# A vision tower with a mixture of experts on one core: gate stores moved ahead, the first expert's weights loaded in two parts, two bias additions later, and identity matmuls in TensorE's pauses

## What is computed

```python
h = tok(x)                       # 64 images: 36 patches of 768 -> layernorm -> 256 -> layernorm, class row, positions
h = h + attention(layernorm(h))  # 37 rows of an image see each other, each row but itself
h = h + ffn(layernorm(h))        # 8 experts, 2 per row, capacity 444

# ffn
probs = softmax(x @ router_w + router_b); topv, topi = top_k(probs, 2); topv /= topv.sum()
prio = where(topi.flat == e, topv.flat, -1); pv, pp = top_k(prio, 444)   # for each expert: its 444 best rows
xin = x[pp // 2]; w = pv
out_e = (gelu(xin @ w1[e] + b1[e], exact) @ w2[e] + b2[e]) * w
out[tok] += out_e; out = layernorm(out) * ln_g + ln_b
```

## Time and profile before

| | us |
|---|---|
| median of 3 runs | 414.99 (413.75 to 417.43) |
| profiled execution, its own time | 417.57 |
| its span | 415.7 |
| granted TensorE clock, mean over the span | 0.917 |
| TensorE busy | 348.5 (84%) |
| VectorE busy | 319.1 (77%) |
| ScalarE busy | 254.7 (61%) |
| GpSimd busy | 222.5 (54%) |

### The profile page before, as it was taken

One profiled execution on the slowest core, in us unless ns is written; L12 is line 12 of the kernel. 1 busy time (PEld: TensorE's weight loads), 2 busy tenths in 40 slices (PEclk: granted clock), 3 DMA queues, 4 the chain that ended last, 5 costly groups with the idle time before them and its releaser, 6 DMA issues.

```text
span 415.7 us, 7904 instructions
## 1 busy us (share of the span) xinstructions
PE 348.5 (84%) x2128; PEld 307.8 (74%) x2128; DVE 319.1 (77%) x874; ACT 254.7 (61%) x552; POOL 222.5 (54%) x377
## 2 busy tenths in 40 slices
PE   2799999999999998540038999999999999999960
PEld 0588888887888886230028899999999999999950
DVE  7674778878888877879887655878787878787954
ACT  3255587767868775644700378686868686868620
POOL 4154776666666764430004443057777777645675
PEclk9898999999999999955557699999999999999996
DMA  6641024545454389678812386655858595852221
GB/s 174 188 88 37 30 58 129 147 128 139 126 151 135 95 134 118 163 196 248 39 0 68 115 254 187 184 147 149 231 165 249 151 243 168 244 171 76 62 83 45
DMA packets 49278, 57.29 MB, mean 138 GB/s; under 512 B 12248, under 2 KB 38229, under 8 KB 49244
## 3 DMA queue, kind: packets, MB, share of 16 engines
q1 hardware_dynamic: 42602, 43.11, 40.0%
q0 software_dynamic: 5568, 13.00, 12.0%
q10 hardware_dynamic: 1074, 0.79, 0.7%
HBM read 36.74 MB, written 21.36 MB: 140 GB/s over the span
## 4 chain that ended last, share of the span: by engine, by line
PE 56%; issue 10%; SPq 8%; POOL 8%; DMA 7%; DVE 6%; ACT 3%; ACTq 0%; DVEq 0%; POOLq 0%
PE pz L977 18%; PE pall L994 17%; PE pall L837 5%; DMA x_rows<-gate 5%; PE pall L805 3%; PE pall L812 3%; SPq L456 2%; SPq L450 2%; POOL nrm L1609 2%; PE pall L1005 1%; DMA stage<-in_x 1%; PE pall L963 1%; SPq L509 1%; PE pall L821 1%; PE pz L785 1%
## 5 line engine op out<-in xcount | busy, mean ns | idle before, releaser
L994 PE MATMUL pall<-halves 128*128 128x444 f32 x384 | 88.5, 365 | 0.8 <-DVE halves L1398 0.8
L977 PE MATMUL pz<-halves 128*128 128x444 f32 x384 | 89.1, 368 | 0.0
L977 PEld LDWEIGHTS pz<-halves 128*128 128x128 f32 x384 | 73.6, 192 | 5.0
L994 PEld LDWEIGHTS pall<-halves 128*128 128x128 f32 x384 | 70.8, 188 | 6.0 <-DVE halves L1398 1.1
L1649 POOL DMA_INDIRECT held<-x_rows,gidx x32 | 35.8, 1119 | 64.3 <-issue 50.4
L738 ACT ACTIVATE wproj<-pz,b1t 128x444 f32<-128x444 f32 x64 | 40.5, 633 | 45.3 <-PE pz L977 44.7
L1398 DVE TENSOR_TENSOR halves<-wproj,halves 128x444 fp32r<-128x444 f32 x64 | 39.8, 622 | 28.2 <-ACT halves L750 22.1
L837 PE MATMUL pall<-halves 128*112 128x256 f32 x396 | 56.6, 299 | 3.2 <-DVE halves L1089 3.2
L837 PEld LDWEIGHTS pall<-halves 128*112 128x112 f32 x396 | 51.3, 183 | 5.1 <-DVE zbias L1108 2.4
L1673 POOL DMA_INDIRECT out<-rows,didx x28 | 37.0, 1323 | 22.7 <-DVE rows L1446 15.4
L750 ACT CAST halves<-wproj 128x444 fp32r<-128x444 f32 x64 | 36.1, 564 | 2.0
(11 more groups left out here) (283 smaller groups left out, 716.4 us busy)
## 6 DMA issues: line engine op xcount, KB each, us to landing
stage<-in_w SPq DMA_DIRECT2D x32, 512.0 KB
stage<-in_x SPq DMA_DIRECT2D x64, 108.0 KB
x_rows<-x SPq DMA_DIRECT2D x22, 224.0 KB, 3.1
x_rows<-held SPq DMA_DIRECT2D x22, 224.0 KB, 4.2
sums<-rows SPq DMA_DIRECT2D x7, 448.0 KB
out<-held SPq DMA_DIRECT2D x21, 111.0 KB
x_rows<-zero SPq DMA_DIRECT2D x1, 1474.9 KB
wproj<-in_w_proj ACTq DMA_DIRECT2D x1, 768.0 KB
```

Of the source, the lines that this page charges most:

```text
L977: m = nc.tensor.matmul(bank(k % 2)[:, 0:CAP], w[:, c, k * 128:(k + 1) * 128], xs[:, e % 2, c, 0:CAP], start=(n == 0), stop=(n == 3 * EC - 1))
L994: m = nc.tensor.matmul(pall[:, 2 * (e % 2) + o, 0:CAP], w[:, k, o * 128:(o + 1) * 128], hs[:, k % 2, 0:CAP], start=(k == 0 and n == 0), st ...
```

## The change

1. SP stores the first 16 tiles' gates at the head of step 25 (TILES + 3), ahead of that step's three stores, and no longer behind the weights.
2. SP loads the first halves of w1 and w2 of expert 0 at the head of step 26, ahead of the last two tiles' `hb` and output stores. The last six tiles' gates are stored after the pipeline; the second halves of w1 and w2 follow them.
3. GpSimd adds the bias row (L1624) for tiles 18 and 19 in step 23; for tiles 20 and 21 in step 26, after a new wait for `r_V` = 2. Before, it did 18 in step 23, 19 and 20 in step 25, and 21 in step 26.
4. TensorE multiplies the identity (128x128, fp32, results into a bank that nobody reads then) 4, 5 + 2, 3 and 8 times in steps 22 to 25, 24 times between L906 and L912, 10 times ahead of the search, 9 times behind each of its first seven rounds, 2 times behind L922, 17 times behind L927, and 16 times (before: 24) behind L932.

```diff
 # SP, in step(i, slot), ahead of the stores
+                if isinstance(i, int) and i == TILES + 3:
+                    sp.wait_ge(r_V, 1)
+                    store_gates(0, EARLY)
+                if isinstance(i, int) and i == TILES + 4:
+                    sp.wait_ge(x_n, TILES)
+                    sp.wait_ge(xT_ps, TILES)
+                    sp.wait_ge(z_ps, TILES)
+                    load_w1(0, 0)
+                    load_w2(0, 0)
...
 # SP, after the pipeline
-            for h in range(2):
-                load_w1(0, h)
-                load_w2(0, h)
-            for a, b, n in ((0, EARLY, 1), (EARLY, TILES, 2)):
-                sp.wait_ge(r_V, n)
-                store_gates(a, b)
+            sp.wait_ge(r_V, 2)
+            store_gates(EARLY, TILES)
+            load_w1(0, 1)
+            load_w2(0, 1)
...
 # TensorE
+            def keep_clock(n, b):
+                for _ in range(n):
+                    nc.tensor.matmul(bank(b)[:, 0:128], ident[:, :], ident[:, :], start=True, stop=True)
...
+                if isinstance(i, int) and i >= TILES:
+                    keep_clock({TILES + 1: 5, TILES + 2: 3, TILES + 3: 8}.get(i, 0), 0)
...
+                if isinstance(i, int) and i >= TILES:
+                    keep_clock({TILES: 4, TILES + 1: 2}.get(i, 0), 0)
...
+            keep_clock(24, 6)
             for t in range(TILES - EARLY):
...
+            keep_clock(10, 7)
             for r in range(NR):
                 pe.wait_ge(r_won, r + 1)
                 nc.tensor.matmul(bank(r % 2)[:, 0:1], grp[:, :], won[:, :], start=True, stop=True).then_inc(r_n, 1)
+                keep_clock(9 if r < NR - 1 else 0, 7)
             pe.wait_ge(r_pick, 1)
             nc.tensor.matmul(bank(2)[0:P, 0:E], onesf[:, 0:P], thrrow[:, :], start=True, stop=True).then_inc(r_thr, 1)
+            keep_clock(2, 7)
...
             nc.tensor.matmul(bank(3)[0:P, 0:n], below[0:P, 0:P], gev, start=True, stop=True).then_inc(r_pos, 1)
+            keep_clock(17, 7)
...
-            keep_clock(24)
+            keep_clock(16, 7)
             for h in range(2):
                 first_gathered(h)
                 lists(h)
...
 # GpSimd, in step(i, slot)
-                for t in range(i - 6, i - 4) if isinstance(i, int) and i == TILES + 3 else (i - 5,):
-                    if live(t) and not (isinstance(i, int) and i == TILES + 2):
+                if isinstance(i, int) and i == TILES + 4:
+                    pool.wait_ge(r_V, 2)
+                for t in {TILES + 1: (i - 5, i - 4), TILES + 2: (), TILES + 3: (), TILES + 4: (i - 6, i - 5)}.get(i, (i - 5,)) \
+                        if isinstance(i, int) else (i - 5,):
+                    if live(t):
```

More of the change, by code:

```diff
@@ L475, in _, with load_w1, load_w2 @@
                 load_x(t, t)
+            HALF_H, HALF_K = HID // 2, HC // 2
+            def load_w1(e, h):
+                cols = slice(h * HALF_H, (h + 1) * HALF_H)
+                sp.dma_start(w1r[:, :, cols], w1[e].rearrange("(c p) h -> p c h", p=128)[:, :, cols])\
+                    .then_inc(w1_in[h], 16)
+            def load_w2(e, h):
+                ks = slice(h * HALF_K, (h + 1) * HALF_K)
+                sp.dma_start(w2r[:, ks, :], w2[e].rearrange("(k p) o -> p k o", p=128)[:, ks, :])\
+                    .then_inc(w2_in[h], 16)
             def step(i, slot):
                 par = slot % 2
+                if isinstance(i, int) and i == TILES + 3:
[7 more added lines that the diff above has]
+                    load_w2(0, 0)
                 t = i + 4
@@ L934, in _ @@
             m.then_inc(r_list, 1)
-            def keep_clock(n):
-                for _ in range(n):
-                    nc.tensor.matmul(bank(3)[:, 0:128], ident[:, :], ident[:, :], start=True, stop=True)
             def lists(h):
```

## The result

The changed kernel takes 423.76 us (median of 6 runs, 422.45 to 425.37), the kernel before, run beside it, 414.37: the ratio is 1.0238 (95% interval 1.0199 to 1.0277), 2.4% slower. One of the six executions of the kernel before took 1890.57 us, which nothing here explains; the other five took 411.26 to 417.43. The forecast was 416.4 with a range up to 420.2. The profiled execution took 422.45 with a span of 420.5.

What follows compares the result with a forecast made beforehand. The gate stores held the first gather by 2.0 us, with the search behind. Round 4 +2.8, products +1.4, sums -0.3, L922 and L926 -0.5, gate wait -2.0 gave +1.4 us: 416.4, range 409.8 to 420.2.

Steps and rivals of the forecast that it cites:

- When w1's half lands: On SP's queue, w1's first half lands at 200.5: pieces through at 198.3, plus 2.2 for stores and weights.
- rival 2: Gate pieces, stores and weights land all in series, w1 at 204: +4.9 us, time 419.9; chance 0.18.
- Round 4: In the search, ScalarE waits for w1, so this round's sum comes at 202.8, +2.8 us.
- The products at half clock: On TensorE, the clock falls in the pause; nine products behind round 4 make round 5 late by +1.4 us.
- Full clock on the later sums: In the search, three later sums get shorter at full clock, -0.3 us; L922 and L926 give a further -0.5.
- The gate wait: Ahead of GpSimd's first gather, the wait for the gate stores goes, giving 2.0 us.
- The sum: Over the whole path: row numbers +3.4, at 222.3; less 2.0 us, the first gather and all the rest +1.4 us.
- The first expert: At the first twelve expert matmuls, the half clock stays as before: 0, between -1.5 and +1.5 us.
- The difference of the medians: For the whole kernel, the profiled execution's +1.4 us carries over to the median of 414.99, giving 416.4.
- Part 3: GpSimd's moved bias-row additions: 0 within ScalarE's wait, -1.0 to +1.0 us if there is no wait.
- Rival 1: On SP's queue, weights come no later than before and everything fits: gather -4.9 us, time 410.1; chance 0.35.
- Rival 3: On TensorE, the products do not hold the clock: +0.5 us in all, about 415.5; chance 0.07.

Runs made afterwards that it cites:

- e1: The kernel before with only SP's new order of DMAs, no products, additions as before: 423.1 us, ratio 1.0161 to the kernel before.
- e6: The changed kernel with 8 tiles' gates stored early instead of 16, the other 14 late: 417.84 us, ratio 1.0063 to the kernel before.
- e4: The changed kernel with the first halves of w1 and w2 issued just ahead of the early gates: 413.82 us, ratio 0.997 to the kernel before.
- e9: e8 with the first halves of w1 and w2 issued in step 23: 412.45 us, ratio 0.9954 to the kernel before.
- e2: The kernel before with TensorE's identity products alone: 415.3 us, ratio 1.0009 to the kernel before.
- e5: The kernel before, unchanged, run once more for a second profile: 416.81 us in the profiled execution.
- e3: The kernel before with GpSimd's new order of additions alone: 415.26 us, ratio 1.0002 to the kernel before.
- e8: e4 with 27 products instead of 16 in the last group, 4 and 3 more behind gathered blocks one and three: 412.58 us, ratio 0.9953.
- e10: e9 with TensorE's program of the kernel before (no products but the 24): 412.65 us, ratio 0.9959 to the kernel before.
- e7: The changed kernel with the two first weight halves issued by ScalarE behind its count of round 0, not by SP: 414.75 us, ratio 1.0001.

## Why the prediction was wrong

The mechanism was read from the trace in the right place (ScalarE's conversion in round 3 waits for w1, the clock falls in the pause, one round is long, the gather then follows the row numbers), but I gave it a size at which the gate wait paid for most of it, and I carried a difference over from one execution to a median. The steps, in profiled executions:

- **When w1's half lands**, predicted 200.5, measured 204.5. This is the step that failed, and it is worth all of the 3.9 us by which the row numbers missed. Two terms of it were too small. I let the pieces take 13.3 us from 185.0 (through at 198.3); the second gate DMA landed at 200.7, though the pieces began sooner, at about 183 (944 packets under 512 B from 183 to 184): some 18 us in place of 13.3, beside the stores. And I added 2.2 for three stores and the weights, "since stores can flow while the pieces drain"; from the gates' landing to w1's were 3.8. The stores do flow, but slowly: from 192 to 200 the DMAs moved 0.73 MB, 92 GB/s, where it was 368 GB/s in the earlier trace rows. "All in series", which I had worked out as 204.2 and filed under rival 2, was right to 0.3 us, in part by luck: the pieces were through 2.4 us later than it says, the two of the three stores whose landing the profile shows took 1.3 us more (to 202.0) and not 3.4, and only its 2.5 for the weights was right. That w1 comes no sooner than the pieces ahead of it in its queue is what e1, e6 and the changed kernel show; SP's late issue (192.7, after 7.53 us at the gates and 3.21 at the next store, 0.82 before) does not set it.
- **Round 4**: predicted +2.8, measured +6.8 (206.81 against 199.99), which follows from the landing.
- **The products at half clock**: predicted +1.4, measured +0.9 (3.55 us from round 4 to 5 against 2.65), since the clock came back at 209.8, while the nine were still running (after 3.0 us of products, where I had 5.2). Right in kind.
- **Full clock on the later sums**: predicted -0.3, measured 0: the two rounds from the sum of round 5 to that of round 7 took 6.15 us after and 6.17 before. For L922, L926 and the rest I had -0.5; from the last sum to the row numbers it was 9.73 against 10.09, -0.36.
- **The gate wait**: predicted -2.0, measured -3.1. I had taken 1.35 us from the row numbers to the gather also when nothing else is late; it is 0.31 (226.24 to 226.55). In the eleven profiles that show both, the first gather starts 1.2 us after the landing of the last gates or 0.3 after the row numbers, whichever is later (221.07 to 222.27 before, 214.89 to 216.09 in e4, 217.01 to 218.21 in e9). So the gates cost the kernel before 3.1 us and not the 2.0 that I put in bold.
- **The sum**: row numbers +7.3 (predicted +3.4), gather +4.3 (predicted +1.4), the profiled execution +4.9.
- **The first expert**: predicted 0, measured 0. From its first hidden to its first project matmul it is 4.63 us in both (232.90 to 237.53, 237.78 to 242.41).
- **The difference of the medians**, 9.4, is 4.5 more than that of the profiled executions. I had carried the difference over from an execution that was 2.6 us above the median and wrote that it carries over. It does not, and this took the result out of my range: with the measured +4.9 in place of +1.4 the same sum gives 419.9, still inside it. Of the 4.5 us, 3.2 are the profiled execution of the kernel before above the median beside the changed kernel (417.57 against 414.37), and 1.3 the changed kernel's profiled execution under its own median (422.45 is the fastest of its six). Where the weights come early, as in e2, the old order has its gather at 217.2, and its runs spread over 6.2 us; in the two profiles of the new order ScalarE waits 9 us for w1, and the six runs of the changed kernel lie within 2.9 us (422.45 to 425.37), none of them near the old median. That the old order is often fast because its weights are early, and the new one never, is likely from the table under e5, with four profiles of the old order and two of the new, but it is not shown run by run.
- **Part 3 and the products** cost and give nothing by themselves (e2, e3), as forecast.
- **Rival 1** (410.1) is the way that e4, e8, e9 and e10 went, once the weights do not stand behind the pieces, but their medians are 412.5 to 413.8: the gather comes at 216 to 218, and against the kernel before that gives 1.5 to 3.1 us and not 4.9.
- **Rival 2** is what came, from one execution to the other: +4.9 predicted, +4.9 measured, with round 4 at +6.3 against +6.8 and the gate wait at -2.0 against -3.1. Its time, 419.9, missed by 3.9 for the same carried difference.
- **Rival 3** did not come: the clock was held up to the wait.

The rule of the Trainium skill that I weighed (DMA: Bandwidth & Descriptors, Queues, rings and completion order) set w1 at 198.3 at the earliest, and 204.5 agrees with it. In e7 a load on another queue landed at 194.6, while pieces of SP's queue were still being sent; the profile does not show which of them an engine had taken before the load, so e7 neither bears the rule out nor speaks against it.

## What to carry to other kernels

A DMA that moves forward in a queue moves all that it passes back: price it by the pieces of the slowest kind that come to stand ahead of the next needed load, in series with it: here w1 landed 3.5 to 3.9 us after the last of them, whenever it had been issued. Put what an engine will wait for ahead of them, and well ahead: just ahead of the pieces it was as slow as behind them. Before a difference is carried from a profiled execution to a median, see whether that execution waited for something that others do not wait for. Work that only keeps TensorE's clock up is worth what the next bound leaves of it: here the rounds were as long with full clock as with half, and 148 products gave 0.2 us, far inside what a measurement can tell.

## What was not expected of the hardware

- 4-byte pieces hold up the issuing engine too: two DMAs of 7 KB took SP 7.53 us to issue, with 15.6 us (median of the two) to landing; 3.5 KB each took 2.66 us and 9.3. In the kernel before, the same pair held SP for 7.7 us as well (1.93 and 5.76), but nothing that was needed soon stood behind it.

```profile
x_rows<-gate SPq DMA_DIRECT2D x2, 7.0 KB, 15.6
```

- The bf16 sum of one column is no faster for the search at full clock: the rounds are 2.57 us apart at half (before: 189.01, 191.57, 194.15) and 2.57 at full clock (after: 188.10, 190.67, 193.25).
- Loads of 512 KB on ScalarE's queue overtake pieces that wait in SP's, at the price of some 10 to 14 us to landing instead of 7.6. On SP's own queue, just ahead of the pieces, w1 pays nearly the same: 11.1 us in e4, 11.8 in e8, against 7.3 in e9.
